# Rotary angles moved from the products to their input, residual adds moved from DMA to TensorE, and all instruction orders rewritten

## The chip, the cores and the metric

The kernel runs on one core of a Trainium2 chip. The core has four compute engines that each work through their own list of instructions in order: TensorE (PE, matrix products and transposes into the eight banks of PSUM), VectorE (DVE), ScalarE (ACT) and GpSimd (POOL). SyncE (SP) and, here, POOL and ACT too issue DMAs. Engines wait for each other through semaphores. The metric is the device time of one launch in microseconds (us), lower is better: the median of several runs.

## The reference, cut to what matters

32 sequences of 256 tokens with 128 channels, all in float32, pass through two transformer layers with conditioning ("adaLN": scales, shifts and gates per sequence from a small vector c). In order:

- Layer 0 attention: normalise and modulate x to h. q, k, v = h times Wq, Wk, Wv, 32 heads of 4 channels. Rotary embedding on q and k: with the two halves u1, u2 of a head's channels, `[u1*cos - u2*sin, u1*sin + u2*cos]`, where the angle depends on the token and on which of 2 frequencies the channel has. phi = elu + 1 of both. Then a linear recurrence over tokens with two decay rates per head: state = state*beta + phi_k*v, key sum likewise; output = (phi_q · state)/(phi_q · key sum), mixed over the two rates. Output projection, layer norm, gate, and a residual add: x1 = x + ...
- Layer 0 FFN: normalise and modulate x1, quantise it blockwise to FP4 values, gate and up products (352 columns), silu(gate)*up, quantise that, down product, gate, residual: x2 = x1 + ...
- Layer 1 attention (RWKV style): normalise, modulate, normalise again, products with token shift, a running-maximum recurrence and two scans, a channel mix with relu squared, gate, residual: x3 = x2 + ...
- Layer 1 FFN as in layer 0: x4 = x3 + ..., which is the result.

## The kernel before, in words

Two sequences form a pair: 512 tokens, in four row tiles of 128. There are 16 pairs. Each pair passes through four stages, named by the first letter of the step functions: a (layer 0 attention), b with layer 0 (its FFN), c (layer 1 attention), b with layer 1 (its FFN). The kernel is software-pipelined by hand. Every engine has a function `body(n)` that lists steps with `do(step, n - k, ...)`: in body n the a steps work mostly on pair n, the layer 0 FFN on pair n-1, the c steps on pair n-2 and the layer 1 FFN on pair n-3. `turns` (L345) runs body(0) to body(5), a loop for n = 6 to 15 and body(16) to body(19). So every engine does the same list once per pair, and the order in `body` (ACT from L789, PE from L1345, DVE from L1750, POOL from L468) is what sets the order of the work. Which PSUM bank a product uses is in the table `BANK`; before it overwrites a bank, a PE step waits (`freed`, `freed_at_ends`) for the last reader of what was there.

The steps that the change touches:

- **q and k.** PE `a2` multiplies h (in columns, `hcol[0]`) by four weight tiles `wqk`: Wq, Wq with the halves of each head swapped, and the same for Wk. That is four products of 128 by 512 tokens into two pairs of banks. DVE `a2` (L1566) multiplies a pair of banks by cos and sin (1024 elements per partition) into `rope`, DVE `a2r` (L1571) adds the two halves to `qk`. ACT `a2` takes exp of the negative part, and DVE `a2p` (L1576) makes phi of both. DVE `a3` multiplies v by phi_k, `a4d` and `a4` (L1591) are the scans, `a4m` (L1617) multiplies the state by the query's share; `a5`, `a5q` make that share.
- **Residuals.** For x1, x3 and x4 PE transposes the branch's columns to rows (L1040, four transposes), ACT copies them to a buffer (`urow`, `arow`, `drow`; it gathers row sums for the first two), and POOL starts a DMA that adds the buffer to `xa` or `xb` in SBUF (`add_x1`, `add_x3`, `add_x4`, L456, L461, L466). For x2 PE does the add itself: `b6x_0` multiplies the old rows by the identity (`rows_of`, L1031) and `b6r_0` accumulates the four column tiles (`add_columns`, L1035) into the same bank; ACT copies the sum out. The next steps, ACT `b1v` (sum of squares, L525), `c1v` (the same for x2) and the normalising `b1n` and `c1n` (L515), wait for these and for POOL's power of -1/2 (L423 to L427).
- **FFN.** DVE `b1m`/`b1q` quantise the input (L1427 to L1441 with `xblk`), DVE `b3` multiplies gate by up (L1663), `b4`/`b4q` quantise the hidden rows (the same lines with `hid`, 1408 elements). PE `b5` transposes them, `b5d` is the down product, ACT `b6g` gates it.
- **Layer 1 attention.** DVE `c4a` (L1690, L1696) starts the running maximum from PE `c3`; ACT `c4`, `c4e` make the exponentials, DVE `c4b` (L1702) needs the first of them.
- **Store.** ACT issues the DMA of the result near the top of its body (`store`, L882); four activation table loads stand at fixed places of the body (L824, L830, L842, L855), also in body(19), which has only the last store and no other step.

## Time and profile before

| | |
|---|---|
| time, median of 3 runs | 1453.92 us (1448.1 to 1456.07) |
| the profiled execution's own time | 1457.73 us |
| its span, first to last instruction | 1454.8 us |
| PE busy | 1157.6 us (80%) |
| DVE busy | 1134.4 us (78%) |
| ACT busy | 1059.1 us (73%) |
| POOL busy | 264.5 us (18%) |
| mean granted clock | 0.899 |
| chain that ended last, by engine | DVE 26%, PE 23%, issue 22%, ACT 20%, POOL 6%, DMA 2% |

Busy is the time in which an instruction of the engine ran; the span is what all of them share. The granted clock is a fraction of 2.4 GHz, the higher of TensorE's two levels. "Issue" in the chain is time with no cause that the profile shows. Three engines are busy for three quarters or more of the span and none for all of it, so the totals alone don't say what bounds the kernel; the rows below are from single stretches.

### The profile page before, as it was taken

Reading aid. Unit: us, or ns where it says so; the run is one execution under the profiler, and the core shown is the slowest. Engines: PE = TensorE matmul, PEld = TensorE weight load, DVE = VectorE, ACT = ScalarE, POOL = GpSimd, SP = SyncE. Lnnn points to the kernel's source line nnn. Section 1 sums busy time; section 2 is a strip of 40 time slices with the busy share of each in tenths; the row PEclk is TensorE's granted clock in tenths of the full one; section 3 lists DMA queues with packets and bytes.
Section 4 is the critical chain, followed back from the end, with each engine's and each line's share of the span. In section 5 each row is a group of like instructions: output and inputs, shape, how many; then the busy total and the mean of one; then the engine's idle time right before and its main releaser. Section 6 shows DMA issues by size and latency. Waiting matters only on the chain.

```text
span 1454.8 us, 18749 instructions
## 1 busy us (share of the span) xinstructions
PE 1157.6 (80%) x5194; PEld 706.2 (49%) x5194; DVE 1134.4 (78%) x1637; ACT 1059.1 (73%) x2849; POOL 264.5 (18%) x382
## 2 busy tenths in 40 slices
PE   5375878989797888889897988889897979878653
PEld 3133444645455554646454555546464555546332
DVE  6758595969798897969797988969797979864613
ACT  4153857779696969777796969687877969677553
POOL 1001121021212111130213122211303121211000
PEclk9676988989899999989899989999899989989776
DMA  4000000010101010100101010101001010101010
GB/s 127 0 8 8 8 15 8 9 29 1 30 8 30 8 30 9 30 7 7 29 0 30 7 29 7 30 7 22 15 7 26 4 29 8 22 8 23 0 22 15
DMA packets 28360, 25.84 MB, mean 18 GB/s; under 512 B 2304, under 2 KB 21376, under 8 KB 28288
## 3 DMA queue, kind: packets, MB, share of 16 engines
q0 software_dynamic: 6912, 12.59, 5.0%
q1 hardware_dynamic: 12928, 8.29, 1.9%
q10 hardware_dynamic: 8448, 4.20, 0.9%
q8 instruction: 22, 0.36, 0.1%
q14 instruction: 50, 0.41, 0.1%
HBM read 8.28 MB, written 4.19 MB: 9 GB/s over the span
## 4 chain that ended last, share of the span: by engine, by line
DVE 26%; PE 23%; issue 22%; ACT 20%; POOL 6%; DMA 2%; ACTq 1%; SPq 0%; DVEq 0%; POOLq 0%
PE ps L923 4%; PE ps L1236 3%; DVE hid L1440 3%; ACT hq L525 2%; PE ps L1125 2%; DVE hid L1663 2%; DVE blk L1427 2%; DVE outer L1582 2%; DVE state L1591 2%; PE ps L1202 2%; PE ps L996 2%; DVE hid L1441 2%; ACT norm L515 2%; POOL rstd_of_f L425 2%; DVE hid L1433 2%
## 5 line engine op out<-in xcount | busy, mean ns | idle before, releaser
L1125 PE MATMUL ps<-wguT,hqcol 128*128 128x352 f32 x512 | 179.8, 483 | 17.7 <-ACT th L708 7.4
L1591 DVE TENSOR_TENSOR_SCAN state<-beta,outer 128x512 f32<-128x512 f32 x128 | 148.3, 1199 | 0.0
L1125 PEld LDWEIGHTS ps<-wguT,hqcol 128*128 128x128 f32 x512 | 93.8, 197 | 86.1 <-issue 25.1
L1440 DVE SCALAR_TENSOR_TENSOR hid<-hidcol,hid 128x1408 f32<-128x1408 f32 (+1 forms) x68 | 106.4, 1569 | 11.3 <-ACT hidcol L717 10.7
L923 PE MATMUL ps<-const,hq 128*128 128x128 f32 x128 | 37.8, 386 | 88.5 <-ACT hq L515 88.4
L1427 DVE TENSOR_REDUCE xblk<-ps 128x32 f32<-128x512 f32 x32 | 22.0, 687 | 100.2 <-PE ps L1063 100.2
L1236 PE MATMUL ps<-hidcol,wdT 128*128 128x256 f32 (+1 forms) x384 | 92.6, 392 | 0.0
L1663 DVE TENSOR_TENSOR hid<-th,ps 128x352 f32<-128x352 f32 x128 | 63.1, 514 | 25.6 <-PE ps L1125 17.3
L1236 PEld LDWEIGHTS ps<-hidcol,wdT 128*128 128x128 f32 (+1 forms) x384 | 73.8, 196 | 18.7 <-issue 6.7
L996 PE MATMUL ps<-state,const 128*32 128x512 f32 x256 | 74.0, 884 | 7.2 <-DVE state L1617 7.1
L1617 DVE TENSOR_TENSOR state<-state,rope 128x1024 f32<-128x1024 f32 x64 | 75.0, 1213 | 1.7
L923 PEld LDWEIGHTS ps<-const,hq 128*128 128x128 f32 x128 | 20.4, 163 | 114.9 <-issue 67.5
L923 PE MATMUL ps<-const,norm 128*128 128x128 f32 x256 | 65.5, 341 | 12.6 <-ACT norm L515 7.0
L708 ACT ACTIVATE th<-ps 128x352 f32<-128x352 f32 x128 | 57.8, 465 | 17.7 <-DVE hid L1663 9.0
L1202 PE MATMUL ps<-const,hid 128*128 128x128 f32 (+1 forms) x384 | 52.5, 290 | 21.7 <-DVE hid L1441 21.7
L1566 DVE TENSOR_TENSOR rope<-ps,const 128x1024 f32<-128x1024 f32 x32 | 38.8, 1212 | 39.0 <-PE ps L940 39.0
L717 ACT ACTIVATE hidcol<-hid 128x1408 f32<-128x1408 f32 x32 | 44.1, 1378 | 34.0 <-DVE hid L1433 34.0
L923 PEld LDWEIGHTS ps<-const,norm 128*128 128x128 f32 x256 | 37.1, 150 | 65.3 <-issue 36.6
L465 POOL TENSOR_TENSOR pool_scrap<-minus_half,eps_tile 128x4 f32<-128x4 f32 x16 | 7.4, 465 | 335.1 <-ACT drow L621 335.1
L1690 DVE TENSOR_TENSOR_SCAN epst<-neg_w,ps 128x256 f32<-128x256 f32 x32 | 20.2, 674 | 59.7 <-PE ps L1275 59.7
L940 PE MATMUL ps<-hcol,wqk 128*128 128x512 f32 x128 | 64.2, 631 | 1.3 <-ACT hcol L660 1.3
L1330 PE MATMUL ps<-xk,fw_key 128*128 128x512 f32 x128 | 63.8, 604 | 0.0
(242 smaller groups left out, 3331.8 us busy)
## 6 DMA issues: line engine op xcount, KB each, us to landing
xa<-in_x SPq DMA_DIRECT2D x16, 256.0 KB, 2.9
xa<-zn POOLq DMA_DIRECT2D x16, 256.0 KB, 3.3
xb<-arow POOLq DMA_DIRECT2D x16, 256.0 KB, 3.3
xb<-drow POOLq DMA_DIRECT2D x16, 256.0 KB, 3.3
out<-xb ACTq DMA_DIRECT2D x16, 256.0 KB, 2.3
const<-in_const SPq DMA_DIRECT2D x1, 848.0 KB, 7.1
state<-in_wmod SPq DMA_DIRECT2D x1, 768.0 KB, 4.8
wqk<-in_wqk SPq DMA_DIRECT2D x1, 256.0 KB, 4.5
```

Of the source, the lines that this page charges most:

```text
L708: s.activation(th[l][:, t % 2, :], bank(f"f{l}_g{t}")[:, 0:I_FF], ACT.Silu).then_inc(s_th[l], 1)
L923: last = t_.transpose(dst[:, t * P:(t + 1) * P], src[:, t, :], ident)
L940: ins = t_.matmul(two_banks(("a_k", "a_q")[h])[:, n_, :], wqk[:, k, :], hcol[0][:, :], start=True, stop=True)
L996: last = t_.matmul(bank("a_n")[c * NH:(c + 1) * NH, :], cst("sel_num"), state[:, m, c, :], start=(m == 0), stop=(m == M - 1), tile_positio ...
L1125: t_.matmul(bank(f"f{l}_{'gu'[g]}{t}")[:, 0:I_FF], hqcol[l][:, t * P:(t + 1) * P], wguT[:, l, g, :], start=True, stop=True).then_inc(s_gu[ ...
L1202: last = t_.transpose(bank(f"f{l}_h{k}{'aac'[c]}")[0:rn, col:col + P], hid[l][:, 2 * k + t, r0:r0 + rn], ident)
L1236: last = t_.matmul(bank(f"f{l}_d")[:, toks], wdT[0:rn, l, c, :], hidcol[l][0:rn, c, toks], start=(c == 0), stop=(c == 2))
L1330: t_.matmul(bank(f"c_f{c}"), fw_key[:, c * P:(c + 1) * P], xk[:, :], start=True, stop=True).then_inc(s_fk_mm, 1)
L1440: return v.scalar_tensor_tensor(dst, mag, low, dst, ALU.max, (ALU.add, ALU.subtract)[part])
L1591: return v.tensor_tensor_scan(state[:, m, c, :], beta[:, m, :], src, 0.0, ALU.mult, ALU.add)
L1617: v.tensor_tensor(state[:, m, 2 * h:2 * h + 2, :], state[:, m, 2 * h:2 * h + 2, :], qshare[:, m:m + 1, :].to_broadcast([P, 2, TOK]), ALU.m ...
L1663: v.tensor_tensor(hid[l][:, t, :], th[l][:, t % 2, :], bank(f"f{l}_u{t}")[:, 0:I_FF], ALU.mult).then_inc(s_hid[l], 1)
```

## The change

Three things, and what follows from them.

1. DVE `a2x` multiplies `hcol[0]` by cos and sin of both frequencies (4 x 256 elements per sequence, twice a pair) ahead of the products. PE `a2` then accumulates Wq·(h cos) and the signed, swapped Wq·(h sin) in PSUM, for each frequency apart: eight products with 64 output columns, the two frequencies in the two halves of the partitions. The channel order within a head row changes accordingly (`h = row % 64 // 2`), and the weights are reordered at the start on DVE. DVE `a2r` is gone; ACT `a2` and DVE `a2p` read the bank. `eqk` and `qshare` get their own memory.
2. x1, x3 and x4 are added on PE like x2. `add_x1`, `add_x3`, `add_x4` and their buffers are gone; ACT writes the sums straight to `xa` and `xb`.
3. `body` of PE, ACT, DVE and POOL has a new order, with new `BANK` numbers and new waits for banks. The cut of the body is elsewhere (a body now starts with what was its middle, so labels are one pair later); the distance between the stages stays.

```diff
-BANK = {"a_b0": 5, "a_b1": 0, "a_den": 6, "a_k": 3, ...
+BANK = {"a_b0": 0, "a_b1": 7, "a_den": 1, "a_fk": 0, "a_fq": 1, ...
...
-    cos = np.tile(np.cos(freqs), (1, SEQ)).astype(np.float32)
-    sin = np.tile(sign * np.sin(freqs), (1, SEQ)).astype(np.float32)
+    turns_of = np.stack([np.cos(freqs), np.sin(freqs)], 1).reshape(1, 2 * (D // 2) * T)
+    angles = np.tile(turns_of, (P, 1)).astype(np.float32)
...
 # POOL
-            def add_x1(i):
-                pool.wait_ge(s_urow, i + 1)
-                g.tensor_tensor(pool_scrap[:, 0, :], minus_half[:, :], eps_tile[:, :], ALU.mult)
-                g.dma_start(of_pair(xa, i), urow[:, :, :], accum_op=ALU.add).then_inc(s_x1, 16)
...
             def body(n):
+                do(power_b1, n - 3)
+                do(power_z0, n - 2)
                 do(power_f0, n - 2)
                 do(power_c1, n - 3)
-                do(add_x4, n - 4)
-                do(add_x3, n - 3)
                 do(power_f1, n - 3)
                 do(power_a1, n - 2)
-                do(power_b1, n - 2)
                 do(power_a0, n)
-                do(power_z0, n - 1)
-                do(add_x1, n - 1)
...
 # ACT
             def a8(i):
-                act.wait_ge(s_urowT, i + 1)
-                rows_out("f0", i, "a_x1", urow, s_urow)
+                act.wait_ge(s_x1mm, i + 1)
+                rows_out("f0", i, "a_x1", of_pair(xa, i), s_x1)
...
             def body(n):          # from the middle of the new list
...
+                do(layer(b5, 0), n - 2, 0)
+                do(layer(b6c, 1), n - 4)
+                do(a3t, n - 1)
+                do(store, n - 4)
+                do(layer(b5, 0), n - 2, 1)
+                do(c8, n - 3)
+                do(a1b, n - 1)
+                do(layer(b6g, 0), n - 2, 0)
+                do(layer(b6g, 0), n - 2, 1)
+                do(layer(b1v, 1), n - 3)
+                do(layer(b6c, 0), n - 2)
+                do(c1v, n - 2)
+                do(layer(b1n, 1), n - 3)
...
 # PE
             def a2(i, h):
-                after(pe, s_hcol[0], i, SEQ)
+                after(pe, s_turned, i, SEQ)
...
+                dst = bank(("a_fk", "a_fq")[h])
                 for n_, k in enumerate(((2, 3), (0, 1))[h]):
-                    ins = t_.matmul(two_banks(("a_k", "a_q")[h])[:, n_, :], wqk[:, k, :], hcol[0][:, :], start=True, stop=True)
+                    for f in range(2):
+                        ins = t_.matmul(dst[f * 64:(f + 1) * 64, :], wqk[:, k, f, :], rope[:, 2 * f + n_, :], start=(n_ == 0), stop=(n_ == 1))
...
             def c8(j):
                 after(pe, s_ag, j, SEQ)
-                rows_from(bank("c_x3"), acol).then_inc(s_arowT, 1)
+                rows_of(bank("c_x3"), of_pair(xb, j))
+                add_columns(bank("c_x3"), acol).then_inc(s_x3mm, 1)
...
 # DVE
-            def a2(i, h):
-                k = 1 - h
-                after(dve, s_qk_mm, i, 2, h + 1)
-                v.tensor_tensor(rope[:, 2 * k:2 * k + 2, :], two_banks(("a_k", "a_q")[h]), tab, ALU.mult).then_inc(s_rope_mul, 1)
-
-            def a2r(i, h):
-                k = 1 - h
-                after(dve, s_rope_mul, i, 2, h + 1)
-                v.tensor_tensor(qk[:, k, :], rope[:, 2 * k, :], rope[:, 2 * k + 1, :], ALU.add).then_inc(s_roped, 1)
+            def a2x(i, q):
+                after(dve, s_hcol[0], i, SEQ, q + 1)
+                before(dve, s_qk_mm, i, 2)
+                toks = slice(q * T, (q + 1) * T)
+                v.tensor_tensor(rope[:, :, toks], hcol[0][:, toks].unsqueeze(1).to_broadcast([P, 4, T]), tab, ALU.mult).then_inc(s_turned, 1)
...
             def body(n):          # start and end of the new list
+                do(a2x, n - 1, 0)
+                do(c4a, n - 3, 0)
+                do(c4a, n - 3, 1)
+                do(a2x, n - 1, 1)
+                do(layer(b3, 1), n - 4, 0)
+                do(c4b, n - 3)
...
+                do(a4m, n - 1, 0, 1)
+                do(a1s, n, 0)
...
+                do(a4m, n - 1, 1, 0)
+                do(a4, n - 1, 1, 1)
+                do(a4m, n - 1, 1, 1)
+                do(layer(b1m, 1), n - 3, 0)
...
+                do(layer(b1q, 1), n - 3, 2)
```

In the old order of DVE `c4a` stood between `b1m` and `b1q` of layer 1, the two rope products and adds behind `b1q`, and `a1s` behind all of `a4` and `a4m`. In the old order of PE, `a2` stood in one place with both halves (`b2` of layer 1 between them); in the new one `a2` of k and of q are apart, `c8` stands between the two `b5` of layer 0 instead of behind them, and `b6r_1` ahead of them.

## Rows read from the trace of the kernel before

**Rows 1.** Stretches: length; busy (count) of PE, PEld, DVE, ACT, POOL; clock; DMA share, GB/s.
```profile
80.00:160.00 80.00, 52.11 (x180) 28.66 (x180) 54.48 (x88) 41.87 (x113) 8.88 (x14) 0.74 0.03 7
...
961.60:1041.80 80.20, 69.53 (x324) 42.56 (x323) 69.08 (x98) 64.26 (x178) 16.01 (x23) 0.94 0.08 17
```
**Rows 2.** Chain that ended last, in order of time: start us, us, what.
```profile
108.88 1.53 DVE blk L1427
...
275.44 1.54 DVE blk L1427
...
1238.15 1.54 DVE blk L1427
```
**Rows 3.** DVE in one period: start us, us, line, operation, shapes, idle before.
```profile
966.07 0.69 DVE L1571 TENSOR_TENSOR qk<-rope 128x512 f32<-128x512 f32 x1
966.67 0.15 DVE L1546 SCALAR_TENSOR_TENSOR negm_f<-sums_f,negm_a 128x4 f32<-128x4 f32 x1
967.16 0.69 DVE L1702 TENSOR_TENSOR ex<-ex,ps 128x512 f32<-128x512 f32 x1 [0.33 <-ACT ex L753]
...
1008.57 1.62 DVE L1441 TENSOR_TENSOR hid<-hid,blk 128x1408 f32<-128x1408 f32 x1
...
1034.01 0.69 DVE L1427 TENSOR_REDUCE xblk<-ps 128x32 f32<-128x512 f32 x1 [4.85 <-PE ps L1063]
...
1039.12 1.26 DVE L1690 TENSOR_TENSOR_SCAN epst<-neg_w,ps 128x256 f32<-128x256 f32 x2 [3.01 <-PE ps L1275]
...
1041.09 1.41 DVE L1440 SCALAR_TENSOR_TENSOR hq<-xmag,hq 128x512 f32<-128x512 f32 x2
...
1044.95 1.22 DVE L1566 TENSOR_TENSOR rope<-ps,const 128x1024 f32<-128x1024 f32 x1 [1.73 <-PE ps L940]
```
**Rows 4.** ACT in the same period.
```profile
966.07 1.06 ACT L753 ACTIVATE ex<-ex 128x1024 f32<-128x1024 f32 x1
...
1025.36 1.65 ACT L515 ACTIVATE norm<-xb,shift_of_a,rstd_of_a 128x128 f32<-128x128 f32 x4 [1.67 <-POOL shift_of_a L427]
```
**Rows 5.** POOL in the same period.
```profile
1023.22 1.80 POOL L425 TENSOR_TENSOR rstd_of_a<-var_of_a,minus_half 128x4 f32<-128x4 f32 x1
...
1033.04 1.01 POOL L416 TENSOR_TENSOR rstd_of_a<-var_of_a,minus_half 128x4 f32<-128x4 f32 x1
```
**Rows 6.** PE in the same period (a float32 product is two records).
```profile
962.45 0.60 PE L1040 MATMUL ps<-const,ucol 128*128 128x128 f32 x4
962.89 1.88 PE L940 MATMUL ps<-hcol,wqk 128*128 128x512 f32 x4
964.61 0.60 PE L1120 MATMUL ps<-const,hq 128*128 128x128 f32 x4
...
998.61 0.65 PE L977 MATMUL ps<-hcol,wmix_d 128*64 128x256 f32 x4
999.19 1.12 PE L1330 MATMUL ps<-xk,fw_key 128*128 128x512 f32 x2
...
1016.09 1.16 PE L1035 MATMUL ps<-const,gcol 128*128 128x128 f32 x8 [0.17 <-ACT gcol L660]
...
1022.68 1.54 PE L923 MATMUL ps<-const,hq 128*128 128x128 f32 x4 [4.36 <-ACT hq L515]
...
1030.46 2.92 PE L996 MATMUL ps<-state,const 128*32 128x512 f32 x12
```
**Rows 7.** The end of the chain that ended last.
```profile
1399.18 3.56 DMA xb<-arow
1402.82 1.66 ACT hq L525 x8
...
1445.65 3.30 DMA xb<-drow
1448.97 0.38 ACTq L882
...
1453.25 1.28 ACT L855
```

More of the change, by code:

```diff
@@ L54, in shape_constants @@
     row = np.arange(P)
[L55 removed]
+    h = row % (P // 2) // 2
     ident = np.eye(P, dtype=np.float32)
@@ L618, in b6c @@
                 else:
-                    act.wait_ge(s_drowT, i + 1)
-                    before(act, s_x4, i, 16)
-                    s.activation(drow[:, :, :], bank("f1_x").rearrange("p (t h) -> p t h", h=H), ACT.Copy).then_inc(s_drow, 1)
+                    act.wait_ge(s_x4mm, i + 1)
+                    s.activation(of_pair(xb, i), bank("f1_x").rearrange("p (t h) -> p t h", h=H), ACT.Copy).then_inc(s_x4, 1)
             def c9(j, q):
@@ L664, in a2 @@
                 k = 1 - n_
-                after(act, s_roped, i, 2, n_ + 1)
-                s.activation(eqk[:, k, :], qk[:, k, :], ACT.Relu, scale=-1.0).then_inc(s_nexp, 1)
+                after(act, s_qk_mm, i, 2, n_ + 1)
+                before(act, s_phi, i, 2)
+                s.activation(eqk[:, k, :], bank(("a_fk", "a_fq")[n_]), ACT.Relu, scale=-1.0).then_inc(s_nexp, 1)
                 after(act, s_nexp, i, 2, n_ + 1)
@@ new lines, in body @@
+                do(c4, n - 3, 2)
+                do(c4, n - 3, 3)
+                do(a8, n - 2)
+                do(c4e, n - 3, 1)
+                do(layer(b1v, 0), n - 2)
+                do(a2, n - 1, 0)
+                s.preload_act_table_set("silu_and_others")
+                do(layer(b3, 1), n - 4, 1)
+                do(c3, n - 3)
+                do(layer(b3, 1), n - 4, 2)
+                do(layer(b1n, 0), n - 2)
+                do(layer(b3, 1), n - 4, 3)
+                do(layer(b1c, 0), n - 2, 0)
@@ new lines, in body @@
+                do(layer(b3, 0), n - 2, 1)
+                do(c5m, n - 3)
+                do(layer(b3, 0), n - 2, 2)
+                do(c5n, n - 3)
+                do(c5x, n - 3)
+                do(a3s, n - 1, 1)
+                do(layer(b3, 0), n - 2, 3)
+                do(c6h, n - 3)
+                do(c6, n - 3, 0)
+                do(c6s, n - 3, 0)
+                do(c6, n - 3, 1)
+                do(c6, n - 3, 2)
+                do(c6s, n - 3, 1)
+                do(layer(b5, 1), n - 4, 0)
@@ L790, in body @@
+                do(c6, n - 3, 3)
+                do(c6s, n - 3, 2)
+                do(c6s, n - 3, 3)
+                do(layer(b5, 1), n - 4, 1)
+                do(layer(b4, 0), n - 2)
+                do(a3m, n - 1)
+                do(layer(b6g, 1), n - 4, 0)
+                do(layer(b6g, 1), n - 4, 1)
                 do(c9, n - 3, 0)
@@ new lines, in body @@
+                do(c4s, n - 3, 1)
+                do(c4v, n - 3)
+                do(c4n, n - 3)
+                do(c4p, n - 3)
+                do(a2p, n - 1, 0)
+                at_start(weight_blocks, n - 1, 0, 1, 1)
+                do(a3, n - 1, 0)
+                at_start(weight_blocks, n - 1, 0, 1, 2)
+                do(layer(b3, 1), n - 4, 1)
+                do(layer(b3, 1), n - 4, 2)
+                do(c4t, n - 3)
+                do(layer(b3, 1), n - 4, 3)
+                do(layer(b4, 1), n - 4, 0)
@@ new lines, in body @@
+                do(layer(b1q, 0), n - 2, 0)
+                at_start(weight_blocks, n - 2, 1, 0, 4)
+                do(layer(b1q, 0), n - 2, 1)
+                at_start(weight_blocks, n - 2, 1, 0, 5)
+                do(layer(b1q, 0), n - 2, 2)
+                at_start(weight_blocks, n - 2, 1, 0, 6)
+                do(layer(b4, 1), n - 4, 3)
+                do(a3, n - 1, 1)
+                at_start(weight_blocks, n - 1, 0, 1, 3)
+                do(a4d, n - 1, 0)
+                at_start(weight_blocks, n - 1, 0, 1, 4)
@@ new lines, in body @@
+                do(layer(b4q, 1), n - 4, 2)
+                do(layer(b4, 0), n - 2, 0)
+                at_start(weight_blocks, n - 2, 1, 1, 2)
+                do(a2p, n - 1, 1)
+                at_start(weight_blocks, n - 1, 0, 1, 5)
+                do(layer(b4, 0), n - 2, 1)
+                at_start(weight_blocks, n - 2, 1, 1, 3)
+                do(a3b, n - 1, 1)
+                at_start(weight_blocks, n - 1, 0, 1, 6)
+                do(layer(b4, 0), n - 2, 2)
+                at_start(weight_blocks, n - 2, 1, 1, 4)
@@ L1751, in body @@
+                do(layer(b4q, 0), n - 2, 2)
+                at_start(weight_blocks, n - 2, 1, 1, 8)
+                do(a4, n - 1, 0, 0)
+                at_start(late_weights, n - 1)
+                do(a5, n - 1, 0)
                 do(a4, n - 1, 0, 1)
+                do(a5, n - 1, 1)
+                do(mean_f1, n - 3)
                 do(a5, n - 1, 2)
-                do(mean_f1, n - 3)
                 do(a4, n - 1, 1, 0)
```

705 lines of the change are left out of this document (297 added, 408 removed), and 10 rows, old and new, of the table BANK.

## The prediction
> **What bounds the kernel now.** I first looked at the busy totals: three engines between 73% and 80%, so none of them bounds all of it. The view by stretches says more: in a full period PE is busy 69.5 us, DVE 69.1 and ACT 64.3 of 80.2 us, and PE's clock is high (0.94) [rows 1]. The chain of waits gives the period itself: the same DVE reduction (the hidden blocks of the layer 0 FFN, L1427) comes at 275.44 and, 12 periods later, at 1238.15 us, 80.2 us each; the two periods before, from 108.88, took 83.3 each [rows 2]. So 14 periods carry 1129 us of the span of 1454.8, and the rest is the first 109 us and the last 217.
>
> Then I went through DVE in order of time over one period. From 967.16 to 1029 it has next to no gap. What idles is one short zone: 4.85 us before the layer 1 input reduction, 3.01 before `c4a`, 1.73 before the first rope product and 0.33 before `c4b`, together 9.9 us [rows 3]. DVE's work is thus 80.2 - 9.9 = 70.3 us of the period, small bubbles included. The zone is a loop through the other engines: when DVE ends the quantised hidden rows (call that T0 = 1010.1, the row at 1008.57), they pass PE, ACT, PE (x2), ACT (sum of squares), POOL, ACT, PE, ACT, PE, ACT, POOL, ACT, PE, ACT, PE until DVE gets `c4a`'s product at 1039.12: 29.0 us. In that time DVE has 29.0 - 7.9 = 21.1 us of other work and then waits. PE waits in the same loop, 4.36 us for ACT's normalised rows [rows 6], and ACT 1.67 us for POOL [rows 4]. The kernel is bound by DVE's work plus what this loop leaves uncovered.
>
> **The change part by part.**
>
> *Rope on DVE.* The two products of 1024 elements remain (both operands now in SBUF; the old ones read PSUM). Two additions of 512 elements go; one takes 0.60 us until the next instruction starts [rows 3]. So DVE's work is 70.3 - 1.2 = 69.1 us. `mean_f0` and `mean_f1` stay one small instruction each. That an operand in PSUM or SBUF makes a difference is bounded by the page: L1566 from PSUM has a mean of 1212 ns, L1617 with both in SBUF 1213; I take nothing.
>
> POOL's power takes 1.80 us at 1023.22, while DVE runs instructions with two SBUF operands, and 1.01 us at 1033.04, while DVE idles [rows 5]. The Trainium skill, "GPSIMD Engine Reference", table row "SBUF interfaces", says that GpSimd shares its SBUF interface with VectorE and is held up when VectorE has two SBUF inputs. By that rule `a2x`, which has two where the old product had one, speaks against the change: POOL's power of the z norm beside it would take 0.8 us more, up to 14 x 0.8 = 11 us in the sum. The trace agrees with the rule; the sum below leaves it out, since DVE's other work in the zone slows POOL just so already.
>
> *Products on PE.* Four products of 512 columns take 4 x 0.86 = 3.4 us now (two in 964.61 - 962.89 = 1.72) [rows 6]. The new eight have 64 output columns each, neighbours in different halves. If two run side by side they take 3.4 us, if not 6.9. The nearest rows: six products with 32 output columns take 2.92 us, where one after another would be 5.2; two with 64 columns and 256 tokens start at 998.61 and the next product follows at 999.19, 0.58 us, where one after another would be 0.86 and side by side 0.43 [rows 6]. I take side by side, and 0.15 us at each of the two visits: +0.3; the other end is +3.4.
>
> The Trainium skill, "TensorEngine Tiling (Array Packing)", section Key Properties, says that a change of the tiling mode drains TensorE. The 0.15 us above agrees with a drain of that size; no run here shows a larger one.
>
> *Residuals on PE.* Each of three adds replaces four transposes (962.89 - 962.45 = 0.44 us) by one product of the rows, 0.86, and four accumulating ones, up to 1.16 less the overlap, 0.9: +1.3 us, three times +3.9 [rows 6]. PE goes from 69.5 to 73.7 us. It lies in PE's own waits as long as the period stays above that; two adds lie near the loop. `b6r_1` stands in front of `b5` but its input is ready before T0, so it is hidden. `c8` stands between the two halves of `b5`: 1.3 us more there, less the 0.4 us for which the second half waits for ACT's copy anyway; I count +1.0 on the loop.
>
> *Off POOL and DMA.* x1, x3 and x4 no longer pass DMA. For x3 the add costs 3.56 us by itself, then 0.1 to the reader [rows 7]. In the steady state nobody but `b1v` waits for it, and that matters for the order: `b1v` of layer 1, four squares with sums, 1.6 us [rows 7], stood behind the copy of x2 and ahead of `c1v` on ACT, in the loop. It now stands ahead of the copy, in ACT's wait for PE. That takes up to 1.6 us off the loop. ACT's other work doesn't change (the copy of `drow` becomes one into `xb`).
>
> *The new order of DVE.* In the loop DVE now has, ahead of `c4a`, also `b1q` of layer 1 (2.1 us, from 1041.09 into its wait) and the first `a2x` (1.1): 21.1 + 3.2 = 24.3 us. The loop is 29.0 + 1.0 - 1.6 = 28.4. Uncovered: 4.1 us. From the end of `c4a` (1041.1) to `c4b`, DVE now has 1.1 (`a2x`) and 0.4 (`b3`); the other side is two ACT relus, a table load and the exp of 1.06 us [rows 4], 3.7 us in all by their means: uncovered 2.1. Old `c4b` came 6.2 us behind `c4a`, so this stretch is shorter, but it is also emptier. Idle 4.1 + 2.1 = 6.2 instead of 9.9. Further along ACT and PE have their new lists; ACT has 80.2 - 64.3 = 15.9 us of slack there and PE 80.2 - 73.7 = 6.5, and I add 0.9 us for stalls that I can't follow (0 to 3.7, which would be all that was won). Period: 69.1 + 6.2 + 0.9 = 76.2 us, that is -4.0. Over 14 periods -56 us.
>
> *Start and end.* Start: eight scalings and six more copies of weights on DVE ahead of everything, 0.1 to 0.2 us each (the four copies to `wv_rep`, L1454, take 0.16 each in the chain): +2. End: pair 15 passes each add once with nothing to hide it. x3: 3.6 less 1.3, -2.3, and once more for pair 14, whose add shared POOL's queue with the x4 add: -3; x4: 3.3 less 1.3, -2; x1 -2. The last store is issued at 1448.97 and four table loads follow it until 1454.5 [rows 7]; with `store` behind them all, the end is 2.3 us (the store's median landing) after the issue: -3. Sum: 2 - 12.3, about -10 (from -3 to -16).
>
> **The sum**, against the profiled execution: 1457.7 - 56 - 10 = 1392 us. That execution is 3.8 us above the median of the runs, so the forecast for the median is 1388 us, 4.5% faster.
>
> **The rivals.**
>
> *The idle closes nearly all.* The new order may overlap more than my walk through it: idle 3 us instead of 7.1, period 72.1, -113 us, -10 at the ends: 1331. For it: a period of 72 still exceeds ACT's 64.3. Against: PE needs 73.7 by its busy time, though some of that is slow only because ACT feeds it (four transposes took 1.54 us at 1022.68 instead of 0.44 [rows 6]).
>
> *The idle only moves.* The loop is as long as before and the new order leaves 9.9 us in other places; only DVE's 1.2 us per period and the ends count: 1453.9 - 17 - 10 = 1427. For it: the loop crosses engines some fifteen times and only 0.6 us of it goes. Against: 3.2 us of DVE work demonstrably moves into it.
>
> *TensorE becomes the bound, and the kernel slower.* The eight 64-column products run one after another: PE 69.5 + 3.9 + 0.3 + 3.4 = 77.1 us, and of its waits the 4.36 us for the normalised rows can't be filled in order; with 1 us of others, 82.5, +2.3 per period: +32 - 10, 1476. It decides from where PE's sum plus that wait exceeds 80.2, that is once the edits cost PE over 5.3 us. For it: PE has the least slack of the three, and all that is taken off DVE and DMA lands on it. Against: the 2.92 us for six narrow products, and that 69.5 contains stretched records.
>
> *PE balances it.* A milder form of the last: the period stays within a microsecond of the old and the ends are eaten by the start, 1454 (no difference).
>
> **How the numbers follow.** My forecast 0.57 (its own range 1360 to 1412); idle only moves 0.18; idle closes 0.11; PE balances 0.06; TensorE bound 0.08. The range for 8 in 10 reaches from 1340, inside the closing case, to 1432, over the moving case. A difference of 0.5% (7.3 us) is about what a measurement of this kernel can tell from none. Faster: 0.57 + 0.18 + 0.11 = 0.86; within: 0.06; slower: 0.08.
>
> **What the changed profile would show.** The period between two hidden-block reductions 75 to 78 us; DVE busy 1.2 us less per period with its idle near 7; DVE waits mostly before `c4a` and `c4b`; PE busy 73 to 74 us a period; the new `a2` pair of four products in about 1.8 us, not 3.5; the copy of x3 followed directly by its squares; the last store at the end of the span. The forecast is wrong if PE's list shows no gaps (rival three), or if DVE's idle per period is still 9 us or more, in particular behind the exp in front of `c4b` or in front of `a2p`, which now waits for ACT's read of a bank and for `a2` placed apart.

## The result, and the profile after

The changed kernel takes 1417.42 us (median of 4 runs, 1417.11 to 1419.27). The kernel before took 1453.09 us (1448.1 to 1456.07) on the same chip: the ratio is 0.9748, 95% interval 0.9727 to 0.9769, so it is 2.5% faster. I had forecast 1388 us and a range of 1340 to 1432: the direction is right and the time lies in the range, but the gain is 36 us, not 66, and 1417.4 is outside the likeliest case's own range (1360 to 1412). The profiled execution took 1419.27 us, with a span of 1417.1. (One execution of one experiment below, the third kernel of 9 to 12, ran at a mean granted clock of 0.725 and took 1642.2 us; it is left out, and nothing is read from its trace.)

The page of the changed kernel, busy time and chain by engine:

```profile
PE 1199.9 (85%) x5610; PEld 723.4 (51%) x5610; DVE 1123.0 (79%) x1619; ACT 1062.4 (75%) x2849; POOL 219.3 (15%) x286
...
PE 63%; ACT 14%; DVE 12%; issue 8%; POOL 2%; SPq 0%; ACTq 0%; DMA 0%; DVEq 0%; POOLq 0%
```

PE has gained 42 us of work, DVE has lost 11, and DMA's share of the chain is 0%, from 2%. "PE 63%" looks as if TensorE had become the bound. An experiment below shows that it has not.

**The pace.** The same reduction as in [rows 2], of the pairs 0, 14 and 15, in DVE's order of time:

```profile
112.57 1.61 DVE L1399 TENSOR_REDUCE blk<-hid 128x88 f32<-128x1408 f32 x1
...
1206.74 1.61 DVE L1399 TENSOR_REDUCE blk<-hid 128x88 f32<-128x1408 f32 x1
...
1284.51 1.61 DVE L1399 TENSOR_REDUCE blk<-hid 128x88 f32<-128x1408 f32 x1
```

The first comes 3.8 us later than before (forecast +2). Fourteen periods take 1094.2 us, before 1129.3: -35.1 (forecast -56). From pair 14's reduction to the end it is 210.4 us, before 216.7: -6.4 (forecast -12.3). The sum is -37.7 on the span.

The periods are not alike, and that is the first thing that I had not foreseen. The first two are 79.3 us each (83.3 before). The other twelve are 76.8, 77.1, 77.6, 79.0, 77.2, 79.1, 77.2, 78.9, 77.2, 80.9, 77.2 and 77.1 us: every second one in the middle is longer. Two neighbours by stretches (columns as in [rows 1]):

```profile
1050.60:1127.80 77.20, 71.57 (x350) 43.20 (x349) 68.19 (x96) 64.24 (x177) 13.89 (x17) 0.98 0.02 7
969.60:1050.60 81.00, 73.06 (x350) 43.81 (x349) 68.36 (x97) 64.58 (x176) 13.18 (x17) 0.94 0.02 7
```

In the undisturbed one DVE idles 9.0 us (11.1 before [rows 1]), in the other 12.6.

**DVE's waits** in the undisturbed period (line, operation, shapes, idle before and what ended it; these answer to [rows 3]). T0 is the end of the first row, 1065.2:

```profile
1063.58 1.63 DVE L1413 TENSOR_TENSOR hid<-hid,blk 128x1408 f32<-128x1408 f32 x1
...
1075.66 0.17 DVE L1529 TENSOR_SCALAR negm_a<-sums_a 128x4 f32<-128x4 f32 x1 [1.20 <-ACT xb L514]
...
1089.49 1.42 DVE L1412 SCALAR_TENSOR_TENSOR hq<-xmag,hq 128x512 f32<-128x512 f32 x2 [1.70 <-ACT xmag L693]
...
1094.53 1.26 DVE L1661 TENSOR_TENSOR_SCAN epst<-neg_w,ps 128x256 f32<-128x256 f32 x2 [1.76 <-PE ps L1251]
...
1100.45 0.69 DVE L1673 TENSOR_TENSOR ex<-ex,ps 128x512 f32<-128x512 f32 x1 [2.31 <-ACT ex L734]
```

With two small ones (0.49 and 0.31) that is 7.8 us, where [rows 3] had 9.9. Three of the waits, 4.7 us, lie between T0 and `c4a`, one (2.3) ahead of `c4b`. I had forecast 4.1 and 2.1. T0 to `c4a` is 29.3 us; it was 29.0, and I had forecast 28.4.

**TensorE in front of the loop.** First the kernel before, then the changed one, both around T0 (1010.1 and 1065.2):

```profile
1010.33 1.50 PE L1202 MATMUL ps<-const,hid 128*128 128x128 f32 x12 [0.47 <-DVE hid L1441]
1011.67 0.60 PE L1040 MATMUL ps<-const,acol 128*128 128x128 f32 x4
1012.22 2.83 PE L1236 MATMUL ps<-hidcol,wdT 128*128 128x256 f32 x12
```

```profile
1064.53 1.02 PE L1012 MATMUL ps<-xb,const 128*128 128x512 f32 x2
1065.39 1.05 PE L1016 MATMUL ps<-const,gcol 128*128 128x128 f32 x8
1066.28 0.82 PE L1180 MATMUL ps<-const,hid 128*128 128x128 f32 x6
1066.93 1.02 PE L1012 MATMUL ps<-xb,const 128*128 128x512 f32 x2
1067.80 1.05 PE L1016 MATMUL ps<-const,acol 128*128 128x128 f32 x8
1068.69 0.82 PE L1180 MATMUL ps<-const,hid 128*128 128x128 f32 x6
1069.34 2.76 PE L1213 MATMUL ps<-hidcol,wdT 128*128 128x256 f32 x12
```

The transposes of the hidden rows (L1202, now L1180) began 0.2 us after T0 and now begin 1.1 after it, because the residual of x4 is still running; the residual of x3 stands between their halves. So the down product begins 4.1 us after T0 instead of 2.1.

**The clock on the loop.** Further along, PE turns columns into centred rows for the next norm (`c1r`), the same eight records in both kernels:

```profile
1028.49 2.04 PE L1264 MATMUL ps<-const,hcol 128*128 128x128 f32 x8 [0.95 <-ACT hcol L660]
```

```profile
1085.69 1.13 PE L1240 MATMUL ps<-const,hcol 128*128 128x128 f32 x8 [0.21 <-ACT hcol L640]
```

From 1026 to 1034 us the granted clock of the old kernel was 0.59, after a wait of 4.36 us on PE; from 1082 to 1090 us the changed kernel had 1.00, after a wait of 2.76. In seven of the old kernel's twelve middle periods the step took 2.04 us or more, in none of the changed kernel's. What a level is worth there, the old kernel shows by itself. In five of its twelve periods the step begins 19.4 to 19.6 us after T0. In four of them it took 1.13 us, and `c4a` came 29.1 us after T0; in the fifth it took 2.05, `c4a` came at 31.0, and that is the old kernel's one long period (82.0 us). Once it both began early (18.2) and took 1.13: `c4a` came at 28.0, and the period was 79.2. So a slow step costs 1.0 to 1.9 us, which makes some 8 us for seven of them: an estimate from these rows of what TensorE's clock adds to the gain. No run separates it from the order.

**The products and the adds** of `a2` and x1, which answer to the first PE rows of [rows 6]:

```profile
1098.29 1.10 PE L1012 MATMUL ps<-xa,const 128*128 128x512 f32 x2
1099.22 1.05 PE L1016 MATMUL ps<-const,ucol 128*128 128x128 f32 x8
1101.07 1.94 PE L924 MATMUL ps<-rope,wqk 128*64 128x512 f32 x8
```

**The end of the loop body.** All of DVE's and ACT's waits on "issue" that add up to something (waited for: us in total, times, longest us). In the kernel before, neither engine has one inside the loop. The changed kernel:

```profile
DVE rope L1542 <- issue: 10.2, 4, 2.7
...
ACT xs L712 <- issue: 6.6, 4, 1.8
```

Four times each (2.5 to 2.7 us on DVE, 1.6 to 1.8 on ACT), in every second period of the loop part: one turn of the loop does two pairs (`body(2 * m)`, `body(2 * m + 1)`, five turns, so four jumps), and there the engines' programs jump back. The body's cut has been moved too, from the top of the old list to `c3`/`a2x`, right in front of `c4a`.

### The profile page after: what moved, and what is told of

Its sections match the earlier page's. It is cut to its first block, busy times and chain, and to the rows that moved or that the text cites. A ratio compares the mean times of both kernels' runs of the same rounds, so it can differ in the third digit from the quotient of the medians.

```text
span 1417.1 us, 19485 instructions
## 1 busy us (share of the span) xinstructions
PE 1199.9 (85%) x5610; PEld 723.4 (51%) x5610; DVE 1123.0 (79%) x1619; ACT 1062.4 (75%) x2849; POOL 219.3 (15%) x286
## 4 chain that ended last, share of the span: by engine, by line
PE 63%; ACT 14%; DVE 12%; issue 8%; POOL 2%; SPq 0%; ACTq 0%; DMA 0%; DVEq 0%; POOLq 0%
PE ps L1101 11%; PE ps L1213 6%; PE ps L1310 4%; PE ps L924 4%; PE ps L1303 4%; PE ps L1180 3%; PE ps L1012 3%; PE ps L1016 3%; PE ps L1250 3%; PE ps L904 3%; PE ps L1251 2%; ACT hq L507 2%; PE ps L977 2%; PE ps L938 2%; POOL rstd_of_a L416 2%
## 5 line engine op out<-in xcount | busy, mean ns | idle before, releaser
L1101 PE MATMUL ps<-wguT,hqcol 128*128 128x352 f32 x512 | 175.4, 485 | 20.5 <-ACT hqcol L681 12.5
L1101 PEld LDWEIGHTS ps<-wguT,hqcol 128*128 128x128 f32 x512 | 97.0, 199 | 82.1 <-issue 30.8
L423 POOL TENSOR_TENSOR var_of_f<-squares_f,eps_sum 128x4 f32<-128x4 f32 x32 | 11.9, 373 | 670.2 <-ACT hq L507 670.2
L1634 DVE TENSOR_TENSOR hid<-th,ps 128x352 f32<-128x352 f32 x128 | 63.4, 512 | 32.1 <-PE ps L1101 19.6
L1588 DVE TENSOR_TENSOR state<-state,qshare 128x1024 f32<-128x1024 f32 x64 | 76.8, 1222 | 2.2
L705 ACT ACTIVATE hidcol<-ps 128x512 f32<-128x512 f32 x64 | 38.1, 595 | 51.9 <-PE ps L1180 51.9
L1213 PEld LDWEIGHTS ps<-hidcol,wdT 128*128 128x128 f32 (+1 forms) x384 | 71.6, 196 | 8.9 <-ACT hidcol L707 0.2
L640 ACT ACTIVATE gcol<-ps,mod_cols 128x256 f32<-128x256 f32 x64 | 26.8, 470 | 61.7 <-PE ps L1213 61.2
L1412 DVE SCALAR_TENSOR_TENSOR hq<-xmag,hq 128x512 f32<-128x512 f32 x64 | 44.3, 692 | 33.7 <-ACT xmag L693 31.4
L1180 PE MATMUL ps<-const,hid 128*128 128x128 f32 (+1 forms) x384 | 55.3, 283 | 18.3 <-DVE hid L1413 17.1
L924 PE MATMUL ps<-rope,wqk 128*64 128x512 f32 x256 | 64.5, 626 | 1.7 <-DVE rope L1542 1.7
L1180 PEld LDWEIGHTS ps<-const,hid 128*128 128x128 f32 (+1 forms) x384 | 44.8, 141 | 38.7 <-issue 37.3
L1250 PE MATMUL ps<-xs,w_mixed 128*128 128x512 f32 x96 | 54.4, 650 | 10.3 <-ACT xs L712 10.3
L1310 PE MATMUL ps<-fw_val,ex 128*128 128x128 f32 x512 | 61.4, 278 | 1.3 <-ACT ex L760 1.3
L1310 PEld LDWEIGHTS ps<-fw_val,ex 128*128 128x128 f32 x512 | 58.4, 192 | 7.3 <-issue 5.0
```

The lines of the kernel that those rows point to most:

```text
L924: ins = t_.matmul(dst[f * 64:(f + 1) * 64, :], wqk[:, k, f, :], rope[:, 2 * f + n_, :], start=(n_ == 0), stop=(n_ == 1))
L1101: t_.matmul(bank(f"f{l}_{'gu'[g]}{t}")[:, 0:I_FF], hqcol[l][:, t * P:(t + 1) * P], wguT[:, l, g, :], start=True, stop=True).then_inc(s_gu[ ...
L1180: last = t_.transpose(bank(f"f{l}_h{k}{'aac'[c]}")[0:rn, col:col + P], hid[l][:, 2 * k + t, r0:r0 + rn], ident)
L1213: last = t_.matmul(bank(f"f{l}_d")[:, toks], wdT[0:rn, l, c, :], hidcol[l][0:rn, c, toks], start=(c == 0), stop=(c == 2))
L1250: t_.matmul(dst, w_mixed[:, k, 0, :], src[:, :, 1:T + 1], start=True, stop=False)
L1310: last = t_.matmul(bank("c_vk")[:, t * P:(t + 1) * P], fkr[:, c, t * P:(t + 1) * P], fw_val[:, c, :], start=(c == 0), stop=(c == F4 // P - 1))
```

## The experiments

All on the changed kernel unless said otherwise. The kernel before ran beside each experiment and had 1455.7 to 1457.5 us, where it had 1453.1 beside the changed kernel; so differences of a few us between experiments depend on whether one compares the times or the ratios. I call a period by the distance of the reductions shown above.

**1. The cut moved.** The part of each body that the change had put ahead of the layer 0 work was put back behind it (one n later, with a return in the last body). The order of the work stays, and so does every instruction.

```diff
 def body(n):                      # DVE; ACT, PE, POOL likewise
-    do(c4a, n - 3, 0)
-    ...
     do(a4, n - 1, 0, 1)
     ...
+    if isinstance(n, int) and n == PAIRS + 3:
+        return
+    do(c4a, n - 2, 0)
+    ...
```

> The new kernel with the same instructions in the same order on every engine; only the place where the loop's body begins and ends is moved, to where the old kernel had it (PE before b5 of layer 0, ACT before c9, DVE before the second a4, POOL before the f1 power). In the trace of the new kernel the period is 77.1 us, but 79.0, 79.1, 79.0 and 80.9 us each time the loop jumps back; DVE waits some 2.5 us for no semaphore before a2x, ACT 1.6 before L712. Theory A (the jump costs because it now lies in the loop through the engines): the four long periods go, -9.5 us, 1408 us. Rival B (every place of the jump costs the same, or the long periods have another cause): 1417 us, within 3.

Measured: 1409.57 us (1406.76 to 1410.76), ratio to before 0.9672 (0.9654 to 0.9691): better than the changed kernel by 0.6% in time (7.9 us) and 0.8% by the ratios. Theory A. The periods are now 76.8 to 77.9 without the long ones; the fourteen together are 7.6 us shorter, and pair 15's reduction comes at 1275.32, 9.2 us earlier. DVE has no wait on issue above 0.2 us left; ACT has one:

```profile
ACT acol L642 <- issue: 4.4, 2, 2.2
```

So the stall at the jump is still there on ACT, at two of the four jumps, in a place where nobody waits for it. What a stall costs depends on where the cut lies. The Trainium skill, "Runtime: NRT & Kernel Launch", section Instruction fetch mechanics, says that a taken branch to a target outside the instruction window must fetch its page first. It gives no time; stalls of 1.6 to 2.7 us at the jumps and nowhere else in the loop part agree with it, but no run here shows the fetch itself. The Trainium skill's "Advanced Engine Details and Errata", section Control Flow Timing, gives about 51 ns for an unconditional branch and about 108 ns for a compare-and-branch; the stalls measured here are far above both.

**2. The old kernel with its cut moved.** The reverse: the old order, jumping back at about the steps where the changed kernel does. It is not quite the same place: DVE now jumps ahead of `a2`, which in the old order stands behind `c4a`, and ACT ahead of the first `c4` (in the changed kernel ahead of `c2`).

```diff
 def body(n):                      # DVE of the kernel before
+    if not (isinstance(n, int) and n == 0):
+        do(a2, n - 1, 0)
+        ...
     do(a4, n - 1, 0, 1)
     ...
-    do(a2, n, 0)
-    ...
```

> The old kernel with its instructions in the same order; only the cut of the loop's body moves, to about where the new kernel has it (DVE before a2, ACT before the first c4, PE before a2, POOL before the b1 power). Theory A: some 2 us at each of four to five jumps, 1453 + 8 to 10 = about 1462 us. Rival B: 1453 us, within 4.

Measured: 1456.5 us (1455.09 to 1460.54), ratio 1.0001 (0.9988 to 1.0014): no difference, rival B. In its trace the periods with a jump are 82.3, 81.2, 82.5 and 81.3 and their neighbours 80.2, 80.9, 80.2 and 79.2. So a jump costs about 1.7 us there as well, but the unrolled periods became shorter than before (79.7, 78.9, 79.1) and the end 3 us shorter. ACT stands on "issue" at each of the four jumps (`ex` L749: 7.9 us in all, the longest 2.1), DVE at none. The stall is seen; that it has a price of its own in the old kernel's total is not.

**3. Without the rows.** TensorE's extra work taken away. This leaves out the addition of the old rows to x1, x3 and x4.

```diff
-                rows_of(bank("c_x3"), of_pair(xb, j))
-                add_columns(bank("c_x3"), acol).then_inc(s_x3mm, 1)
+                rows_from(bank("c_x3"), acol).then_inc(s_x3mm, 1)   # four transposes; x1, x4 likewise
```

> The new kernel, leaving out the residual adds of x1, x3 and x4 (each branch alone is written as transposed rows): TensorE has 1.3 us less at three places, 3.9 us per period; nothing else changes. Theory TensorE (the new period is TensorE's own work plus the one wait that it can't fill): the period falls by 3 to 3.9 us, 1417 - 14 x 3.5 = 1368 us. Rival DVE (DVE's work plus the loop through the engines, in which only one of the adds lies): by up to 1 us per period, 1403 us or more.

Measured: 1396.89 us (1396.21 to 1400.1), ratio 0.9590 (0.9569 to 0.9611). Undisturbed periods are 75.8 to 76.4, one 77.0, instead of 77.1 to 77.2: 1.1 us for 3.9 us of TensorE's work (20.5 us of the whole time for some 62). The theory of TensorE said 1368, so TensorE is not the bound; the rival's "1403 or more" was 6 us too high, since the start and the end became 5 us shorter as well. What went is one gap, the 1.20 us in front of `mean_a1`; the other waits of the zone stayed. DVE in this kernel:

```profile
978.93 2.33 DVE L1564 TENSOR_TENSOR_SCAN state<-beta,outer 128x512 f32<-128x512 f32 x2
981.30 0.17 DVE L1531 TENSOR_SCALAR negm_a<-sums_a 128x4 f32<-128x4 f32 x1
...
995.12 1.42 DVE L1414 SCALAR_TENSOR_TENSOR hq<-xmag,hq 128x512 f32<-128x512 f32 x2 [1.69 <-ACT xmag L693]
```

**4. The two additions back on DVE**, into a tile that nobody reads.

```diff
                 after(dve, s_expqk, i, 2, h + 1)
+                v.tensor_tensor(spare[:, :], rope[:, 0, :], rope[:, 1, :], ALU.add)
```

> The new kernel with two additions of 512 elements per pair put back on DVE, ahead of each a2p (into a tile that nobody reads): what the change took off DVE, 1.2 us per period. Theory TensorE: DVE idles 9 us per period and the additions mostly go into that, 0 to 6 us in all, 1417 to 1423 us. Rival DVE: 1.2 us in each of 16 periods, 1436 us.

Measured: 1435.15 us (1433.4 to 1436.53), ratio 0.9841 (0.9821 to 0.9861). The undisturbed period is 78.4, +1.25 for about 1.2 us of DVE work: one for one, as the theory of DVE said (1436). The additions stand where DVE has next to no gap. Together with the last run: a microsecond added to DVE there costs one, a microsecond taken off TensorE gives back 0.3; adding work to TensorE was not run. DVE's work plus the loop is still the bound, as before.

This run also prices a part of the change: the two additions put back take 17.7 us of the 35.7 us won (13.5 by the ratios), so something like half of the gain is DVE's lighter work. The rest belongs to the order, the residual adds and the clock together.

**5. All three adds back on POOL's DMAs**, in the new order.

```diff
-                rows_of(bank("c_x3"), of_pair(xb, j))
-                add_columns(bank("c_x3"), acol).then_inc(s_x3mm, 1)
+                rows_from(bank("c_x3"), acol).then_inc(s_x3mm, 1)
...
+                do(add_x4, n - 4)      # POOL, behind power_c1
+                do(add_x3, n - 3)
```

> The changed kernel with the three residual additions of x1, x3 and x4 given back to GpSimd's accumulating DMAs (rows copied by ScalarE into arow, urow or drow, added in DRAM-to-SBUF queue order on GpSimd's software queue); the products with multiplied columns, the order and the cuts of the changed kernel stay. Theory A (the loop of VectorE and its own work is the bound; TensorE's extra work costs about 0.3 us per us, as the run without the three additions showed with 1.1 us for 3.9): TensorE loses 3.9 us per period, the pace gains at most 1.1 us per period (-15 us over the run), but each x3 and x4 now lands 3.5 to 4 us after its copy; the end of the run alone gets that back two or three times (+8 to +11 us), and the steady periods lose some of the 1.1: 1405 to 1425, most likely 1415. Theory B (TensorE, 63% of the chain of waits, is the bound): 3.9 us x 14 periods = -55, plus at most 11 at the end: about 1375. Theory C (latency of the DMA sits on the loop, so moving the additions to TensorE was the main gain of the change): slower than the changed kernel by 2 us per period or more: 1440 to 1450.

Measured: 1550.71 us (1550.4 to 1551.35), ratio 1.0648 (1.0626 to 1.0669). All three theories missed. The nearest, C, had the direction, but 1440 to 1450. The chain of waits of this kernel now runs through three DMAs in one period (start us, us):

```profile
422.52 3.33 DMA xa<-zn
469.16 3.36 DMA xb<-drow
475.24 3.28 DMA xb<-arow
508.45 3.36 DMA xa<-zn
```

**6. Only x4 by DMA.** The same edit for x4 alone.

> As the changed kernel, with only the last addition of a layer pair (x4, what the feed-forward network hands to the head) back on GpSimd's accumulating DMA; x1 and x3 stay on TensorE. Theory A (TensorE costs about 0.3 us per us in the steady periods): -1.3 x 0.3 x 14 = -5, and the DMA of the last pair shows its 3.5 us at the end: about 1415, within 4 of the changed kernel. Theory B (TensorE is the bound): -1.3 x 14 = -18 + 3.5: about 1403. Theory C (DMA latency on the loop): slower, 1425 or more.

Measured: 1490.29 us (1489.34 to 1495.04), ratio 1.023 (1.021 to 1.0251), theory C: 73 us for a single add. The period is 81 to 85. ACT's row shows the way:

```profile
958.20 0.60 ACT L714 ACTIVATE hidcol<-ps 128x512 f32<-128x512 f32 x1 [4.86 <-DMA xb<-drow]
```

ACT issues the store of the result. In the new order it stands right behind the copy of x4 and ahead of the second half of the hidden columns, so ACT stands still for the whole DMA, and the loop behind it too. By the kernel's text the store can't simply go later (no run tried it): the copy of x2 waits for the store of the pair whose buffer it takes (`act.wait_ge(s_out[i % 2], ...)` in `b6c`), and that copy is on the loop. In the old order the copy of x4 stood well ahead of the store, and 3.3 us of DMA lay in between unseen. So my comparison is not of "DMA against TensorE" by itself: the new order with the adds on DMA is worse (1550.7 and 1490.3) than both the old kernel and the changed one. How the adds on TensorE would do in the old order was not run.

**7. The cut moved, and the four empty table loads at ACT's start taken out.**

```diff
-            s.preload_act_table_set("natural_log_exp_and_others")   # four of them, ahead of the bodies
```

> The changed kernel with the loop's cut moved off the reduction loop (as in the run with the cut moved), and the four empty table loads at the head of ScalarE's program taken out. The start's first normalise waited for those loads: the first reduction mark should come 1.9 us earlier (112.6 to 110.7) if they are on the path that sets the start (theory A: 1407.5); if the weights' or x's transfers end last there anyway, no change from 1409.6 (theory B).

Measured: 1410.44 us (1409.29 to 1414.36), ratio 0.9682 (0.9662 to 0.9701), like experiment 1. Theory B. The first reduction did not come 1.9 us earlier but 2.7 later than in experiment 1 (115.3 against 112.6), and with the loads out just the same it comes at 112.8 in the first kernel of 9 to 12. So the table loads are not what makes the start later, and single traces differ by more at this mark than what I was looking for.

**8. The copy of x2 ahead of the squares**, on top of 7. This undoes one step of the change.

```diff
-                do(layer(b1v, 1), n - 3)
                 do(layer(b6c, 0), n - 2)
+                do(layer(b1v, 1), n - 3)
```

> As e9_cut_all, with one pair of steps on ScalarE exchanged: the copy of x into rows (b6c of layer 0) goes ahead of the squares of the other layer's normalisation (b1v of layer 1, 1.53 us), which the change had put in front of it. Theory A (the new gap of 1.20 us on VectorE ahead of mean_a1 lies on the loop, as VectorE's own work does): a period gets 0.8 to 1.2 us shorter, 14 x 1.0 = -14 against e9_cut_all: about 1394. Theory B (VectorE waits for something else right behind, the delayed squares or TensorE's products, so that the gap only moves): within 3 us of e9_cut_all. Theory C (the squares are now late for the layer's normalisation chain and cost more than the copy gave): slower than e9_cut_all by 5 us or more.

Measured: 1448.1 us (1445.24 to 1448.74), ratio 0.9936 (0.9914 to 0.9959): 38 us slower than 7, theory C, and by far more than it said. The periods are mostly 79.9 and 80.6 in turn. ACT and POOL in it:

```profile
1016.84 0.28 ACT L516 ACTIVATE xb<-ps 128x128 f32<-128x128 f32 x1 [1.39 <-PE ps L1020]
...
1019.58 1.19 POOL L423 TENSOR_TENSOR var_of_f<-squares_f,eps_sum 128x4 f32<-128x4 f32 x1 [32.75 <-ACT hq L509]
1020.85 1.86 POOL L425 TENSOR_TENSOR rstd_of_f<-var_of_f,minus_half 128x4 f32<-128x4 f32 x1
...
1023.02 1.26 ACT L499 ACTIVATE hq<-xb,shift_of_f,rstd_of_f 128x128 f32<-128x128 f32 x3 [1.99 <-POOL shift_of_f L427]
```

The copy did not come earlier at all: it waits 1.39 us for TensorE, and `mean_a1` keeps its gap (1.15 us). I had read the gap's releaser, the copy on ACT, as being late because of the squares in front of it; it is late because of TensorE. The 1.5 us of squares had simply filled that wait. Moved behind the copy they are 2.5 us later, POOL's steps for them follow in a stretch where they are slow (1.19 and 1.86 us), and ACT waits 1.99 us for the result. DVE then waits 5.05 us for `xmag` where it waited 1.7 to 2.3:

```profile
1035.30 1.42 DVE L1418 SCALAR_TENSOR_TENSOR hq<-xmag,hq 128x512 f32<-128x512 f32 x2 [5.05 <-ACT xmag L695]
```

**9 to 12. Work moved on ACT inside the loop**, all on top of 7. First `a1b`, a copy of 0.73 us, out of the loop's stretch:

```diff
+                do(a1b, n - 1)
                 do(c9, n - 3, 0)
...
                 do(c8, n - 3)
-                do(a1b, n - 1)
```

> As the kernel with the loop's cut moved and without the four table loads (1410.4 us there), with one ScalarE instruction moved: the copy with bias of 512 columns (a1b, 0.73 us) leaves the stretch of 24 us in which ScalarE has next to no idle time (from the hidden rows' transposes to c4a) and goes ahead of c9, where ScalarE waits 1.26 us for TensorE. Theory A (in that stretch ScalarE is what the loop runs on, so 0.73 us less there is 0.5 to 0.7 us less per period): 14 x 0.6 = -8, about 1402. Theory B (the stretch waits for TensorE's gate products and GpSimd's power at the same points; ScalarE's time there is just what fits): no change, 1408 to 1412.

Measured: 1409.73 us (1409.41 to 1412.91), ratio 0.9684 (0.9665 to 0.9704). No change, theory B. The next step on ACT, `b6g`, waits for TensorE anyway: 0.81 us where it waited 0.20.

Then the next pair's normalised rows behind `c1`:

```diff
                 do(c1n, n - 2)
-                do(a1n, n)
                 do(c1, n - 2, 0)
                 do(c1, n - 2, 1)
+                do(a1n, n)
-                do(a1, n, 0)
                 do(c2s, n - 2)
```

(`a1` follows behind `a5y` and `c2n`, and on PE `a1` goes behind `c1r`.)

> As the same kernel, with the normalised rows of the next pair (a1n, four activations of 1.65 us in all, ahead of which ScalarE waits 0.95 us for GpSimd), which nobody on the loop needs, moved from ahead of the two conditioning products' copies of layer 1 (c1) to behind them, its transposes on TensorE likewise. Theory A (1.65 + 0.95 us less on the loop ahead of c1, of which 1.3 come back as a wait for the transposes, and the squares of c2s come 0.6 us earlier): 0.3 to 0.6 us less per period, about 1404. Theory B (what is moved only lands in the next place of the loop): 1408 to 1412. Theory C (the columns of the next pair are then late for the cos/sin products on VectorE): slower, 1415 or more.

Measured: 1427.7 us (1427.44 to 1432.55), ratio 0.9814 (0.9792 to 0.9836): slower, in the range of theory C but not by its way, since DVE doesn't wait ahead of `a2x`. The periods are 78.2 to 78.9, one 80.5. What was moved had only filled ACT's wait for TensorE ahead of `c1`, which is 3.00 us now; `c1` comes no earlier, the moved rows follow behind it, and `xmag` comes 0.7 us later than in 7.

Then both moves together:

> Both moves of the two kernels before. Theory A: the sum of their gains, about 1396. Theory B: no change from 1410. If only one of them gains, that one's time.

Measured: 1429.56 us (1429.26 to 1434.33), ratio 0.9824 (0.9801 to 0.9846): like the second alone.

Last, a useless copy of 512 columns more on ACT in the same stretch:

```diff
                 spread_squares("a1", j, xb, norm[1])
+                s.activation(spare[:, :], hcolb[:, :], ACT.Identity)
```

> As the kernel with the cut moved and without the four table loads, with one useless ScalarE copy of 512 columns (0.7 us) added behind the squares of c1v, inside the stretch. Theory A (ScalarE is what the loop runs on there): +0.6 to +0.7 us per period, 1410.4 + 9 = 1419. Theory B (ScalarE waits in the stretch anyway, 2.7 us in 24, and the copy fits): 1408 to 1413.

Measured: 1417.3 us (1412.93 to 1418.21), ratio 0.973 (0.971 to 0.975). By the median that is 7 us more than 7, but the profiled execution (span 1410.6) has periods of 76.8 to 78.1, on average 77.5 where 7 had 77.3, which makes some 3 us. Between the theories; I don't settle it.

The best version is thus the changed kernel with its cut moved (experiments 1, 7 and the first of 9 to 12 agree within 1 us): 1409.6 us, 3.3% faster than before.

## Why the prediction was right, and where it fell short

- *DVE's work* (forecast -1.2 us per period, to 69.1): busy time fell by 0.7 to 0.9 [rows 1], and the period less the named waits is 69.4 us. Experiment 4 shows that such work counts one for one. Right in kind, 0.3 us too large; why is open.
- *Products side by side* (four in about 1.8 us, not 3.5): L924 has four of 512 columns, eight records, in 1.87 to 1.94 us. Right; the rival in which TensorE becomes the bound and the kernel slower fell with it.
- *TensorE's busy time* (forecast 73.7): 71.6 at a granted clock of 0.98, 73.1 at 0.94, the clock of [rows 1]. Right, and experiment 3 shows that TensorE is not the bound in spite of 63% of the chain.
- *`b6r_1` "so it is hidden"*: this step failed. Its input is ready before T0, as I said, but not early enough: product and accumulation ran from 0.7 us before to 1.1 us after T0 and held up the transposes by 0.9 us. With +1.1 for `c8` (forecast +1.0) the loop carries 2.0 us of residuals. Experiment 3 gets 1.1 of it back per period, the rest is covered by what comes next on the loop.
- *`b1v` "takes up to 1.6 us off the loop"*: the sign is right, and experiment 8 prices the step at 2.9 us per period in the new order, more than I gave it. From the end of x2's copy to the squares of the a norm it was 1.5 us and is 0.4 (0.32 of it a wait for DVE's mean), 1.1 us less, and the 2.0 us of residuals outweigh that. Behind these squares two things nearly cancel: the next pair's rows (`a1n`) now stand ahead of `c1`, and PE's `c1r` takes 0.9 us less at the higher clock. T0 to `c4a` came out at 29.3 instead of 28.4. The clock was in no term of the sum.
- *Idle 7.1 us*: 7.8 in an undisturbed period, 4.1 of it right before `c4a` and `c4b` as forecast, the rest before `mean_a1` and `xmag`'s reader. (The small bubbles, 1.2 us, are counted with the work, as in the prediction.) Undisturbed, the period is 69.4 + 7.8 = 77.2; I had 76.2.
- *The cut of the loop body* was not in my prediction at all, though the diff moves it. It is the second failed step: I took all 14 periods as equal. The four long periods exceed their neighbours by 9.2 us in all; moving the cut gave back 7.6 us of the fourteen periods and 7.9 of the whole time (experiment 1).
- *Power on POOL beside the new product*, the rule on the shared SBUF interface: the z norm's power still took 1.01 us, since it runs behind `a2x`. But the small addition ahead of it runs beside `a2x` and took 0.96 us instead of 0.20, so the 0.8 us of the prediction did come, one instruction earlier. In the four periods in which DVE stood still at the jump the same addition took 0.20:

```profile
1011.21 0.20 POOL L431 TENSOR_TENSOR mean_square_z<-squares_z,eps_tile 128x4 f32<-128x4 f32 x1 [2.50 <-ACT zn L532]
...
1091.86 0.96 POOL L431 TENSOR_TENSOR mean_square_z<-squares_z,eps_tile 128x4 f32<-128x4 f32 x1 [2.50 <-ACT zn L532]
```

ACT waits 0.43 us for this norm. The new order hit another power too: the a0 power, 1.01 us in [rows 5], now runs beside DVE's state product and scans:

```profile
1081.23 1.90 POOL L416 TENSOR_TENSOR rstd_of_a<-var_of_a,minus_half 128x4 f32<-128x4 f32 x1 [0.59 <-DVE var_of_a L1519]
```

ACT waits 0.95 us for it.
- *Start* +3.8 instead of +2. This can't be sized from one trace: the first reduction comes at 112.6 to 115.3 us in four kernels with the same list of work up to there (changed, experiments 1, 7 and the first of 9 to 12), and the old kernel's at 108.8 or, in experiment 2, 110.5. From 60 to 80 us the granted clock was 0.83 in the kernel before, 0.59 in the changed one and 0.61 in experiment 2.
- *End* -6.4 instead of -12.3: from the last copy of x3 to the end the kernel takes 57.0 us before (1397.82 to 1454.8) and 47.9 now (1369.20 to 1417.1), -9.1, with the x3 and x4 DMAs and the table loads behind the store gone:

```profile
1413.83 0.60 ACT L602 ACTIVATE xb<-ps 128x512 f32<-128x512 f32 x1 [2.11 <-PE ps L1016]
1414.46 0.38 ACTq L863 DMA_DIRECT2D out<-xb  x1
```

But from pair 15's reduction to that copy it takes 84.7 us, where it took 81.7. These 3 us are the residuals on TensorE with nothing to hide them: experiment 3, without the rows, has 82.1 us there at nearly the same granted clock (0.83, the changed kernel 0.84). The clock counts too: experiment 1 has 82.4 us with the rows, at 0.90. The prediction had set its 1.3 us for each add against DMAs that took 3.3 to 3.6, and nothing for the stretch before.

In sum: -56 was -35. The first two periods fell by 4.0 us each, as forecast. In the other twelve the undisturbed period is 1.0 longer than forecast (12 us), and the four long ones add 9. -12.3 was -6.4 and +2 was +3.8. The bound, DVE's work plus an uncovered loop, held, and so did the direction; the gain was 36 us instead of 66 because the residuals on the loop were sized at 1.0 us and took 2.0, and the cut of the body was left out.

## What to carry to other kernels

Price each engine by adding and taking away a microsecond of its work before you call it the bound: the share of the chain said TensorE (63%), the runs said DVE (1.0 for 1 added) and not TensorE (0.3 for 1 taken away). Where a hand-ordered loop runs over and over, look where its body jumps back as you would look at any other wait, and put the cut where the engines have slack. A step that fills another step's wait looks like the cause of that wait in the profile; look at what its successor would wait for without it, because exchanging the two here cost 2.7%.

## What the runs showed of the hardware that I had not expected

- ACT and DVE stand still 1.6 to 2.7 us where the program jumps back, in the loop part alone. In the old kernel, which jumps just as often, neither shows such a wait inside the loop; why is open.
- A single step of POOL on 128x4 elements takes 0.20 us or up to 1.19, and its power 1.01 or 1.86 to 2.06. The slow ones in the changed kernel all run beside DVE instructions with both inputs in SBUF, but not each power beside such an instruction is slow (1.01 us at the shortest).
- Four float32 products of 512 columns with 64 output columns, neighbours in different halves of the partitions, take 1.87 to 1.94 us, where four with 128 output columns take 3.4 (two in 1.72 [rows 6]).
- The same eight records of PE take 1.13 us or 2.04, at the higher and at the lower granted clock. Which level they met changed with the order, though the change didn't touch them.
